# A token-mixing block on one Trainium2 core: the expert FFN on pairs of batches, its first layer as fp32 matmuls in two 64-row tiles

## The reference, cut to what matters

```python
def ffn(x, gate_w, gate_b, W1, b1, W2, b2):      # x: [8*1056, 64]; W1: [8, 64, 128]; W2: [8, 128, 64]
    probs = softmax(x @ gate_w + gate_b)
    cw = keep_top2(probs)                         # [tokens, 8], zero for the other six
    for e in range(8):
        h = gelu(x @ W1[e] + b1[e])
        acc += cw[:, e:e+1] * (h @ W2[e] + b2[e])
    return acc
h = h + ffn(layernorm(h))
```

## Time and profile before

| | value |
|---|---|
| median of three runs | 997.62 us |
| profiled execution | 1001.97 us |
| its span in the profile | 1000.2 us |
| PE busy in the span | 899.0 us (90%) |
| DVE, ACT, POOL busy | 573.0, 494.4, 138.7 us |
| granted PE clock, mean | 0.922 of full |
| phase 1 with the wait at its end | 0 to about 759.4 us |
| phase 2 | about 759.4 to 1000.2 us |

### The profile page before, as it was taken

One profiled execution on the slowest core, in us unless ns is written; L12 is line 12 of the kernel. 1 busy time (PEld: TensorE's weight loads), 2 busy tenths in 40 slices (PEclk: granted clock), 3 DMA queues, 4 the chain that ended last, 5 costly groups with the idle time before them and its releaser, 6 DMA issues. The chain is left out here.

```text
span 1000.2 us, 17890 instructions
## 1 busy us (share of the span) xinstructions
PE 899.0 (90%) x5900; PEld 374.9 (37%) x5900; DVE 573.0 (57%) x1201; ACT 494.4 (49%) x1189; POOL 138.7 (14%) x148
## 2 busy tenths in 40 slices
PE   5665899999999989999999999999965989899996
PEld 5241322433342343343243334333412535354443
DVE  4025565578874557876557887788230553636331
ACT  0020254466664536665446676666533454555552
POOL 0010100011010011101001101001000344444443
PEclk9965589899999988999989999999876999999998
DMA  8329351027551005536002305100006655382731
GB/s 153 57 47 163 62 62 31 3 35 119 97 69 44 2 4 67 117 67 110 2 1 30 40 2 68 44 3 1 1 5 141 120 126 117 80 184 52 155 78 22
DMA packets 55864, 64.58 MB, mean 65 GB/s; under 512 B 23893, under 2 KB 41825, under 8 KB 55777
## 3 DMA queue, kind: packets, MB, share of 16 engines
q1 hardware_dynamic: 55777, 63.46, 35.5%
HBM read 36.73 MB, written 2.43 MB: 39 GB/s over the span
## 5 line engine op out<-in xcount | busy, mean ns | idle before, releaser
L887 DVE TENSOR_REDUCE max_parts<-bank 128x1 f32<-128x512 f32 x512 | 329.6, 685 | 137.4 <-PE bank L1075 134.5
L811 ACT ACTIVATE probs<-bank 128x384 f32<-128x384 f32 (+1 forms) x768 | 313.4, 466 | 191.1 <-PE bank L1038 189.6
L1038 PE MATMUL bank<-q_stack,k_stack 99*128 99x384 bf16 (+1 forms) x768 | 229.9, 329 | 4.9 <-ACT probs L811 4.2
L1075 PE MATMUL bank<-k_stack,q_stack 96*128 96x512 bf16 x512 | 208.4, 409 | 17.2 <-DMA k_stack<-part 13.2
L1016 PE MATMUL bank<-probs,v_tiles 128*32 128x384 f32 (+1 forms) x1536 | 160.2, 490 | 5.4 <-ACT heads_out L796 5.0
L1038 PEld LDWEIGHTS bank<-q_stack,k_stack 99*128 99x128 bf16 x768 | 72.2, 99 | 196.1 <-ACT probs L811 146.1
L1285 ACT ACTIVATE hid<-bank,biases 128x352 f32<-128x352 f32 x192 | 96.0, 552 | 84.8 <-PE bank L1329 84.7
L1304 DVE SCALAR_TENSOR_TENSOR prod<-bank,biases,cwb 128x352 f32<-128x352 f32 x96 | 55.8, 582 | 120.1 <-PE bank L1317 103.0
L1329 PE MATMUL bank<-x,w 128*128 128x352 bf16 (+1 forms) x576 | 105.2, 320 | 6.3 <-DMA x<-part 6.3
L1317 PE MATMUL bank<-hid,w_sb 128*64 128x352 f32 x384 | 79.2, 491 | 7.7 <-DVE prod L1304 4.0
L1052 PE MATMUL bank<-x,tok_m 128*64 128x512 f32 x256 | 68.5, 634 | 9.4 <-DMA text_in<-in_txt 8.0
(11 more groups left out here) (146 smaller groups left out, 704.2 us busy)
## 6 DMA issues: line engine op xcount, KB each, us to landing
cwb<-gates_by_expert SPq DMA_DIRECT2D x16, 1056.0 KB, 12.1
x<-in_x SPq DMA_DIRECT2D x64, 256.0 KB, 6.9
q_stack<-part SPq DMA_DIRECT2D x48, 132.0 KB, 6.1
k_stack<-part SPq DMA_DIRECT2D x48, 132.0 KB, 6.6
x<-part SPq DMA_DIRECT2D x32, 132.0 KB, 2.5
h_res<-h_new SPq DMA_DIRECT2D x4, 528.0 KB, 3.0
h_all<-h_res SPq DMA_DIRECT2D x4, 528.0 KB, 3.1
h<-h_all SPq DMA_DIRECT2D x8, 264.0 KB, 3.2
```

Of the source, the lines that this page charges most:

```text
L811: nc.scalar.activation(probs[:, group % 3, h, 0:n], src, ACT.Exp, scale=SCALE).then_inc(exp_done, 1)
L887: nc.vector.tensor_reduce(max_parts[:, c, H * j + h, i % 2:i % 2 + 1], src[:, :], AX.X, ALU.max)\
L1038: last = nc.tensor.matmul(bank[:, 0:n], ks[par][0:ROWS + 3, h, P * kt:P * kt + P], qs[par][0:ROWS + 3, h, QC[qc]], start=True, stop=True)
L1075: last = nc.tensor.matmul(bank[:, :], queries(h, j), ks[par][0:ROWS, h, HALF * (i % 2):HALF * (i % 2) + HALF], start=True, stop=True)
```

## The change

The FFN now works on pairs of batches in the attention's layout. The steps are still 96: one expert, both batches of the pair, one chunk.

- First layer: two fp32 matmuls, batch 0 with rows 0 to 63 of `w1_sb` and `xn2`, batch 1 with rows 64 to 127, into two banks; all 128 output columns each. The bf16 splits of x and of W1, the stacks and their DMAs are gone. x has two buffers (`xn2`).
- One gelu reads both banks (2 x 352 columns). `hid` has three slots.
- Second layer: the same two column tiles, now with the same weights and a batch each.
- DVE: one product per step, `prod` has two slots. POOL: one add per step, the first of a chunk takes `h2_all` directly.
- Gates are loaded per pair in six DMAs, chunk by chunk, each chunk with its own semaphore.
- Output: nine transposing matmuls of `acc` per pair instead of nine folding ones per batch, in three steps (`AT_FOLD`) that share bank 6, each waiting until ACT has read the one before.
- Every engine, DVE too, does the product first and then the norm step. The four pairs are written out, with no hardware loop.
- b2 comes by two DMAs at the start instead of one.

The diff, cut to its core:

```diff
@@ norm
             elif name == "scale":
-                v.tensor_tensor(xn[:, tokens], xc[:, tokens],
+                v.tensor_tensor(xn2[p % 2][:, tokens], xc[:, tokens],
-            elif name == "split":
...
@@ phase 2
-        cwb = [sb(f"cwb{i}", [P, E // 2, L]) for i in range(2)]
-        hid = sb("hid", [P, 4, CH])
-        prod = sb("prod", [P, 4, CH])
+        N_HID, N_PROD, FOLDS, STORES = 3, 2, 3, 5
+        cwb = [sb(f"cwb{i}", [P, E, L]) for i in range(2)]
+        hid = sb("hid", [P, N_HID, 2, CH])
+        prod = sb("prod", [P, N_PROD, CH])
         AT_NORM = {0: [("centre", 0)], 1: [("centre", 1)], 2: [("centre", 2)],
-                   3: [("roots", 0)], 5: [("scale", 0)], 6: [("scale", 1)], 7: [("scale", 2)], 9: [("gates", 0)],
-                   10: [("split", 0), ("choose", 0)], 11: [("split", 1), ("choose", 1)],
-                   12: [("split", 2), ("choose", 2)], 13: [("choose", 3)], 14: [("choose", 4)], 15: [("choose", 5)],
-                   16: [("turn", 0)]}
-        FOLD_LAST, FOLD_FIRST = 8, 20
+                   3: [("roots", 0)], 5: [("scale", 0)], 6: [("scale", 1)], 7: [("scale", 2)], 8: [("gates", 0)],
+                   9: [("choose", 0)], 10: [("choose", 1)], 11: [("choose", 2)], 12: [("choose", 3)],
+                   13: [("choose", 4)], 14: [("choose", 5)], 16: [("turn", 0)]}
+        AT_FOLD = [4, 9, 12]
+        def run_phase2(eng, product, norm_step, fold_step):
+            for p in range(PAIRS):
+                for m in range(PER_PAIR):
+                    c, e = divmod(m, E)
+                    product(p, c, e)
+                    if p + 1 < PAIRS:
+                        for name, i in AT_NORM.get(m, []):
+                            norm_step(eng, name, i, p + 1)
+                    if p > 0 and m in AT_FOLD:
+                        fold_step(p - 1, AT_FOLD.index(m))
@@ SP
+                def load_gates(p):
+                    at_least(sp, y_read, PER_PAIR * (p - 1))
+                    for c in range(NCH):
+                        for bp in range(2):
+                            src = cw_dram.rearrange("e (b l) -> b e l", b=B)[2 * p + bp, :, chunk[c]]
+                            sp.dma_start(cwb[p % 2][D * bp:D * bp + D, :, chunk[c]],
+                                         src.unsqueeze(0).broadcast_to([D, E, CH])).then_inc(cw_loaded[p % 2][c], 16)
...
                 load_gates(0)
+                for p in range(PAIRS):
+                    if p > 0:
+                        store(p - 1)
+                    if p + 1 < PAIRS:
+                        store_gates(sp, p + 1)
+                        load_gates(p + 1)
+                store(PAIRS - 1)
@@ ACT
+                    act.wait_ge(hid_full, n + 1)
+                    at_least(act, y_full, n - N_HID + 1)
+                    first = 2 * (n % 2)
+                    nc.scalar.activation(hid[:, n % N_HID, :, :], psum[:, first:first + 2, 0:CH], ACT.Gelu,
+                                         bias=b1_sb[:, e:e + 1]).then_inc(gelu_done, 1)
@@ DVE
+                    if e == 0:
+                        dve.wait_ge(cw_loaded[p % 2][c], 16 * 2 * (p // 2 + 1))
+                    dve.wait_ge(y_full, n + 1)
+                    at_least(dve, summed, n - N_PROD + 1)
@@ PE
+                def second_layer(n):
+                    p, m = divmod(n, PER_PAIR)
+                    pe.wait_ge(gelu_done, n + 1)
+                    at_least(pe, y_read, n - 1)
+                    for bp in range(2):
+                        last = nc.tensor.matmul(banks[4 + n % 2][D * bp:D * bp + D, 0:CH], w2_sb[:, m % E, :],
+                                                hid[:, n % N_HID, bp, :], start=True, stop=True)
+                    last.then_inc(y_full, 1)
+                def product(p, c, e):
...
+                    at_least(pe, gelu_done, n - 1)
+                    for bp in range(2):
+                        rows = slice(D * bp, D * bp + D)
+                        last = nc.tensor.matmul(banks[2 * (n % 2) + bp][:, 0:CH], w1_sb[rows, e, :],
+                                                xn2[p % 2][rows, chunk[c]], start=True, stop=True)
+                    last.then_inc(hid_full, 1)
+                    if n > 0:
+                        second_layer(n - 1)
+                def fold_step(p, i):
+                    at_least(pe, out_read, FOLDS * p + i)
+                    if i == 0:
+                        pe.wait_ge(summed, PER_PAIR * (p + 1))
+                    if i < 2:
+                        for t in range(4):
+                            first = P * (4 * i + t)
+                            last = nc.tensor.transpose(banks[6][:, P * t:P * t + P], acc[p % 2][:, first:first + P], ident)
+                    else:
+                        last = nc.tensor.transpose(banks[6][0:TXT, 0:P], acc[p % 2][:, IMG:L], ident)
+                    last.then_inc(out_full, 1)
```

More of the change, by code:

```diff
@@ L108 @@
 PV_LAG = 2 * H
-N_SETUP = 11
+N_SETUP = 12
 SHIFT_DMAS = TPC
@@ L179, in build @@
         cw_tail = sb("cw_tail", [2 * E, TXT])
-        banks = [bank(f"bank{i}") for i in range(8)]
+        psum = ctx.enter_context(nc.psum_tensor("bank", [P, 8, 512], F32))
+        banks = [psum[:, i, :] for i in range(8)]
         score_bank = banks[0:3]
@@ L243, in sb1 @@
             return phase1.enter_context(nc.sbuf_tensor(name, shape, dt))
+        qk_part = [sb1(f"part{i}", [P, L], BF16) for i in range(3)]
         xt = [sb1(f"x{i}", [P, NPATCH + 1, 4, V]) for i in range(2)]
@@ new lines, in store @@
+                def store(p):
+                    sp.wait_ge(out_read, FOLDS * (p + 1))
+                    for bp in range(2):
+                        rows = out[2 * p + bp, 0:IMG, :].rearrange("(v t o) c -> o v t c", t=KT, o=2)
+                        for o in range(2):
+                            sp.dma_start(rows[o], outs[p % 2][V * o:V * o + V, :, bp, :]).then_inc(out_stored, 16)
+                    sp.dma_start(out[2 * p:2 * p + 2, IMG:L, :].rearrange("b t c -> t b c"), out_tail[p % 2][:, :, :])\
+                      .then_inc(out_stored, 16)
@@ L1293, in _ @@
                 run_phase2(nc.scalar, product, norm_scalar, evacuate_out)
-                evacuate_out(B - 1, 1, 0)
+                for i in range(FOLDS):
+                    evacuate_out(PAIRS - 1, i)
             @block.vector
             def _(dve):
-                def product(b, bp, c, k, n):
-                    if (c, k) == (0, 0):
-                        dve.wait_ge(cw_loaded[bp], 16 * 2 * (n + 1))
-                    dve.wait_ge(y_full, YPB * b + 4 * c + k + 1)
-                    at_least(dve, summed, YPB * b + 4 * (c - 1) + max(k, 1))
-                    nc.vector.scalar_tensor_tensor(out=prod[:, k, :], in0=banks[4 + k % 2][:, 0:CH], scalar=b2_sb[:, k:k + 1],
-                                           in1=cwb[bp][:, k, chunk[c]], op0=ALU.add, op1=ALU.mult).then_inc(y_read, 1)
@@ L1307, in _, with product @@
-                run_phase2(nc.vector, product, norm_vector, lambda b, bp, fills: None, step_first=True)
+                def product(p, c, e):
+                    n = PER_PAIR * p + E * c + e
+                    if e == 0:
+                        dve.wait_ge(cw_loaded[p % 2][c], 16 * 2 * (p // 2 + 1))
+                    dve.wait_ge(y_full, n + 1)
+                    at_least(dve, summed, n - N_PROD + 1)
+                    nc.vector.scalar_tensor_tensor(out=prod[:, n % N_PROD, :], in0=banks[4 + n % 2][:, 0:CH],
+                                                   scalar=b2_sb[:, e:e + 1], in1=cwb[p % 2][:, e, chunk[c]],
+                                                   op0=ALU.add, op1=ALU.mult).then_inc(y_read, 1)
@@ L1309, in _ @@
+                run_phase2(nc.vector, product, norm_vector, lambda p, i: None)
             @block.tensor
             def _(pe):
-                def experts_out(b, bp, c, k):
-                    pe.wait_ge(gelu_done, KPB * b + E * c + 2 * k + 2)
-                    at_least(pe, y_read, YPB * b + 4 * c + k - 1)
-                    for o in range(2):
-                        e = 2 * k + o
-                        last = nc.tensor.matmul(banks[4 + k % 2][D * o:D * o + D, 0:CH], w2_sb[:, e, :],
-                                                hid[:, e % 4, :], start=True, stop=True)
-                    last.then_inc(y_full, 1)
@@ L1341, in fold_batch @@
-                def fold_batch(b, bp, fills):
-                    pe.wait_ge(norm_read, fills)
-                    at_least(pe, out_read, b)
-                    pe.wait_ge(summed, YPB * (b + 1))
-                    for t in range(KT):
-                        nc.tensor.matmul(banks[6][:, D * t:D * t + D], acc[:, bp, P * t:P * t + P], fold,
-                                         start=True, stop=True)
-                    nc.tensor.matmul(banks[7][0:TXT, 0:D], acc[:, bp, IMG:L], fold, start=True, stop=True)\
-                      .then_inc(out_full, 1)
@@ L1357, in constants @@
+                run_phase2(nc.tensor, product, norm_tensor, fold_step)
```

(3 more changed lines are left out.)

232 lines of the change are left out of this document (49 added, 183 removed).

## The result

The changed kernel takes 992.99 us (median of 20 runs, 988.51 to 1001.08), the kernel before 997.58 us on the same occasions; the ratio is 0.9935, with a 95% interval of 0.9918 to 0.9952. The forecast was 25 us less, the result is 4.6 us less by the medians and 6.5 by the ratio. The way is right, the size is a quarter of what was forecast (by the medians less than a fifth).

The account below looks back on a forecast made before the run. PE was taken to bound phase 2. From 769.7 us, second layers 69.6, first layers 72.7, norm 24.3, folds 7.2, waits 20.1, plus 11.7 at the end, gave 975.3 against 1000.2, 25 less: 973 us, range 959 to 996.

Parts of the forecast that it names:

- The first layer: PE, each step: two fp32 matmuls in row tiles overlap and take 0.79 us instead of 1.00.
- Rivals 1 and 2: First layer: row tiles run in turn, 1022 us, chance 0.14; or only their weight loads don't overlap, 992 us, 0.10.
- Second layer, ACT, DVE, POOL: Each step: second layer stays 0.74 us on PE; gelu 0.55 to 1.10, DVE 0.58, POOL 0.93, all hidden below 1.53.
- Folds: PE, output of each pair: nine transposing matmuls take 2.4 us instead of 4.3.
- The waits of the new order: PE waits at roots, 1.2 us each at scale 1, scale 2, gates, and 2.0 for gelu after Exp; 20.1 in all.
- Gates: Gate loads per pair: chunk 0 is there 14.7 us after the turn, at no cost to PE.
- Rival 4: Gate loads: short runs halve the rate and the gates come late, 995 us; chance 0.05.
- The start: Start of phase 2: product 0 near 768.9 us instead of 775.03, a gain of 6 us.
- The sum: Phase 2: from 769.7 us, 193.9 us of PE work and waits, plus 11.7, give a span of 975.3 us.
- rival 2: First layer: the tiles overlap but their weight loads don't, 1.0 us per step, 992 us in all; chance 0.10.
- rival 3: PE's waits from DVE's order are smaller: half of them and a first layer of 0.74 give 960 us; chance 0.11.
- The end: From the last second layer through output transposes and stores: worked out at 11.3 us, kept at 11.7.

Follow-up runs that it names:

- e1: Changed kernel with DVE doing the norm step before the product again, as before the change: 963.49 us, ratio 0.9633 to the kernel before.
- e2: Changed kernel with twelve unused fp32 matmuls put where PE would wait for DVE, order kept: 986.2 us, ratio 0.987 to the kernel before.
- e4: Changed kernel with a Copy in place of the gates' Exp for the second to fourth pair: 982.41 us, ratio 0.9834 to the kernel before.
- e9: Changed kernel itself, run again beside the filled one on the same chip: 991.33 us, ratio 0.9912 to the kernel before.
- e3: Kernel before the change with one edit, DVE does the product before the norm step: 1035.28 us, ratio 1.0354 to the kernel before.
- e5: e1 with the same twelve filling matmuls as e2: 972.24 us, ratio 0.972 to the kernel before.
- e6: e1 with a Copy in place of the gates' Exp for the second to fourth pair: 960.08 us, ratio 0.9615 to the kernel before.
- e7: e1 with the last pair's three output steps in three banks of their own: 964.33 us, ratio 0.9654 to the kernel before.
- e10: The kernel of e2 once more, beside the changed kernel on the same chip: 986.75 us, ratio 0.9882 to the kernel before.

## Why the prediction was wrong, step by step

**The first layer** (0.79 us taken, 0.74 to 1.37 bounded): right, 0.79 us. Two fp32 matmuls in 64-row tiles take what one takes. Rivals 1 and 2 are out, and so is the estimate of 0.96 us worked out from the Trainium skill's page "TensorE: Matmul & The Clock Gate", section "Part 3: Packing small matmuls — row/col tiling": for two tiles of fp32 the overlap is full here.

**Second layer, ACT, DVE, POOL:** right. The second layer takes 0.74 us. One gelu of 704 columns takes 0.85 us, DVE's product 0.58, POOL's sum 0.93, all hidden in the steady stretch:

```profile
L1190 ACT ACTIVATE hid<-bank,biases 128x704 f32<-128x704 f32 x96 | 81.0, 847 | 102.4 <-PE bank L1242 102.4
```

**Folds:** too dear. Four transposes take 0.59 us at full clock (in e1, 822.36 to 822.95), so a pair needs about 1.4 us rather than 2.4, 3 us less in three pairs.

**The waits of the new order:** right in place and nearly in size. Forecast 14.1 us for scale, gates and roots, measured 13.1; forecast 6.0 for gelu after Exp, measured 6.4. With the mended order e1's phase 2 is 202.0 us. The forecast's own sum for the change, 975.3 - 759.4 = 215.9 us, less those 14.1 us, is 201.8. That it fits to 0.2 us is partly luck: e1 has 6.8 us at 1.2 GHz between start and end, 3.4 us lost, which the sum does not know, and folds that are 3 us cheaper than the sum has them.

**Gates:** right for PE, wrong for DVE. The forecast called a wait for `cwb` in later pairs a sign of being wrong, and it came: DVE waited 2.3, 2.8 and 2.6 us for the gates in the three later pairs (18.8 us in four places, with 11.1 at the start). For the second pair they were there 15.6 us after the turn (813.31 to 828.95), 14.7 forecast. PE's one wait for a product, 0.9 us, is at the start, so the price was nothing, as forecast. Rival 4 is out.

**The start:** product 0 stands 9.8 us after SP's first issue (761.72 to 771.56), forecast 9.5. That issue itself came 2.4 us later than in the profile before. This is not the change: in the profiles of e1, e2 and e4, with the same phase 1, phase 2 starts at 760.2, 755.6 and 756.1 us, and the time at 1.2 GHz in phase 1 is 141, 123 and 123 us (141 in the changed kernel, 133 in the kernel before). The clock varies from execution to execution.

**The sum:** here is the failed step. It set every group and every wait at the full clock, because the earlier trace rows showed 1.00 for the periods before, and it took the 20.1 us of waits to cost 20.1 us. From the third second layer to the end of the last the forecast has 193.9 us; measured are 772.3 to 983.9, 211.6 us. The 17.7 us between them are mostly the clock: of the 53.9 us at 1.2 GHz 16 belong to the start and the end, and half of the other 37 is 19. Against that stand folds 3 us cheaper than forecast; the waits, 20.8 us with 1.3 for the turn, are as forecast, and some 1.5 us I can't place. The rest of the 21.3 us between the profiled span, 996.6, and the forecast 975.3 is 2.4 of phase 1, 0.3 of the start and 1.0 of the end. What could have been seen: in the old profile the one wait for the gates (775.03) was also followed, with a roots group between, by a few microseconds at half clock, from about 780 to 783 us. I put it down to the start and did not ask what nine more waits would do.

**The range** took in 993 us by luck, for reasons that did not come true (rival 2 named 992); **rival 3** (smaller waits) went the wrong way: the waits were as forecast, and taking 13.1 us of them away in e1 took 16.4 us of lost clock with them (11.8 against the trace of e9). Two sums of the rivals are slightly off: half of the 14.1 us is 7, half of the 20.1 is 10, and rival 3 has 8; rival 4 adds up to 996.5, not 995. **The end** took 12.7 us against 11.7 kept.

What stays open: what exactly brings the clock down. Between start and end it fell seven times in the changed kernel: behind the three gates groups, behind one wait for gelu, and behind the three roots groups. Counted over all traces, the wait makes the difference at the gates: right behind a row of waits that ends in one of 1.05 us (the changed kernel, e9, e4) nine of nine gates groups are followed by low clock, seven of them for about 7 us; without it (the kernel before, e1, e2, e3, e5, e6, e7, e10) eight of 24, each for less than 4 us. The roots groups are the open half. In the second and third pair PE does not wait just before them, and still 14 of 15 are followed by low clock in the five traces of the changed kernel with its order (e2, e4, e9 and e10 with it), against four of 15 in the five with the norm step first. In the changed kernel that is 13.6 of the 37 us. Both groups are rows of narrow matmuls (2 and 16 columns), and no run took them out, so how much of the fall is theirs is not shown. What e1, e2 with e10, and e3 show from three sides is that the order costs low clock beside its waits, and that filling the waits gives a part of it back.

## What to carry to other kernels

An engine that runs its own operations ahead of the step that the bounding engine waits for turns slack into a chain: ask of each step, in program order, what stands before it, and place the steps of a side computation before the main product on the engine that serves them. A wait of about one microsecond on a busy TensorE can cost twice its length, as here, where the granted clock fell behind every gates group that stood at the end of a row of such waits and behind a third of those that did not; so read the clock column beside the busy time, and add the low clock to the price of every wait that an edit adds. And when a large saving moves the time little, account for it in three parts (idle, low clock, work at full clock) before doubting the saving itself: here e1 gets 35 us out of the change by moving one engine's order.

## What the runs showed of the hardware that I had not expected

- Two fp32 matmuls of 64 rows, 128 columns of weights and 352 columns of data, in two row tiles, take 0.79 us together, as long as one of 128 rows.
- Filling PE's waits with twelve useless matmuls, 11 us of work, made phase 2 8.2 and 8.7 us shorter.
- The same program took from 983.7 us at a mean granted clock of 0.922 to 996.1 us at 0.904 on one chip (e9), with its neighbours in between in the same order, more or less: the spread of the times is mostly that of the clock.
- A fp32 transposing matmul of 128 x 128 costs 0.15 us in a row of four, where a fp32 matmul against a constant of half the width cost 0.24 (two instructions of 0.12).
